# LSTM with a conditioned adapter on one core: adapter weights from contiguous columns of W2, bias added on VectorE and placed by transfers, two early blocks, end reordered

## What is computed

```python
def lstm(x, h0, Wx, Wh, b):            # x: 16 x 256 x 256
    xz = x @ Wx + b
    for t in range(256):
        ai, af, ao, ag = split(xz[:, t] + h @ Wh, 4)
        c = sigmoid(af) * c + sigmoid(ai) * tanh(ag)
        h = sigmoid(ao) * tanh(c)      # h is the output of step t
x = x + lstm(x, cond, Wx, Wh, b)

def adapter(x, cond, ...):
    c = layernorm(cond) * gamma + beta
    w = gelu(c @ W1 + bias1) @ W2 + bias2            # 16 x 8192
    a1, b1, a2, b2 = [t.reshape(16, 256, 8) for t in split(w, 4)]
    u   = einsum("btd,bdr->btr", x, a2)
    mid = gelu(x @ base_down + einsum("btr,blr->btl", u, b2))
    v   = einsum("blr,btl->btr", b1, mid)
    return mid @ base_up.T + einsum("bkr,btr->btk", a1, v)
x = x + adapter(x, cond, ...)
```

## Time and profile before

| | |
|---|---|
| median of three runs | 617.69 us (616.36 to 618.73) |
| profiled execution | 618.71 us, its span 616.9 us |
| granted TensorE clock, mean | 0.994 of full speed |
| PE, busy share of the span | 97% |
| DVE | 77% |
| ACT | 61% |
| POOL | 6% |
| mean DMA rate over the span | 63 GB/s |

### The profile page before, as it was taken

The page is one execution under the profiler, slowest core; times in us unless marked ns, Lnnn a source line. Parts: engine busy times, 40 slices in busy tenths (PEclk is TensorE's granted clock), DMA queues, the critical chain, the costliest instruction groups (busy, mean ns, idle before and its releaser), DMA issues.

```text
span 616.9 us, 33976 instructions
## 1 busy us (share of the span) xinstructions
PE 600.0 (97%) x14120; PEld 439.0 (71%) x14120; DVE 473.0 (77%) x2543; ACT 375.9 (61%) x2158; POOL 38.6 (6%) x77
## 2 busy tenths in 40 slices
PE   8699999999999999999999999999999999999997
PEld 5565555777777777777777777777777777777886
DVE  3576667888888888888888888888888888888772
ACT  2365555666666666666666666666666666666662
POOL 3000000000000000000000000000000000000000
PEclk9799999999999999999999999999999999999999
DMA  5884630233333113323221233322113323221201
GB/s 161 229 209 157 182 46 15 35 46 55 55 55 54 33 33 49 54 55 54 55 38 37 39 54 55 54 55 44 37 32 55 55 55 55 49 39 25 47 21 35
DMA packets 31499, 38.74 MB, mean 63 GB/s; under 512 B 3632, under 2 KB 29536, under 8 KB 30321
## 3 DMA queue, kind: packets, MB, share of 16 engines
q1 hardware_dynamic: 31282, 36.51, 29.8%
q0 software_dynamic: 64, 0.07, 0.0%
HBM read 15.59 MB, written 4.19 MB: 32 GB/s over the span
## 4 chain that ended last, share of the span: by engine, by line
PE 94%; DVE 2%; DMA 1%; issue 1%; ACT 0%; SPq 0%; ACTq 0%
PE z L696 36%; PE x_bank L494 18%; PE z_o L696 9%; PE aux L520 8%; PE out_bank L543 6%; PE out_bank L625 3%; PE aux L505 3%; PE aux L472 2%; PE out_bank L575 2%; PE aux L527 2%; PE out_bank L564 1%; PE x_bank L564 1%; DMA seed<-proj 1%; PE x_bank L520 1%; DVE z L833 0%
## 5 line engine op out<-in xcount | busy, mean ns | idle before, releaser
L696 PE MATMUL z<-wh,h_t 128*16 128x96 f32 x8160 | 236.5, 249 | 3.4 <-DVE h_t L853 2.0
L696 PEld LDWEIGHTS z<-wh,h_t 128*16 128x16 f32 x8160 | 154.0, 96 | 120.0 <-DVE h_t L853 86.5
L833 DVE STREAM_TRANSPOSE z<-z 128x96 f32<-128x96 f32 x512 | 151.4, 298 | 83.5 <-PE z L696 64.0
L413 ACT ACTIVATE gates<-z 128x48 f32<-128x48 f32 x512 | 107.2, 209 | 127.4 <-DVE z L833 127.3
L494 PE MATMUL x_bank<-wx,x_t 128*128 128x256 f32 x512 | 156.2, 393 | 0.5 <-ACT x_t L331 0.5
L337 ACT ACTIVATE z<-seed 128x96 f32<-128x96 f32 x512 | 127.7, 250 | 5.9 <-DMA seed<-proj 5.8
L696 PE MATMUL z_o<-wh,h_t 128*16 128x64 f32 x4080 | 104.1, 219 | 0.4 <-issue 0.4
L843 DVE SCALAR_TENSOR_TENSOR prod<-gates 128x32 f32<-128x32 f32 x512 | 97.6, 191 | 1.2 <-ACT gates L413 0.3
L341 ACT ACTIVATE z_o<-seed 128x64 f32<-128x64 f32 x256 | 58.3, 228 | 60.5 <-DVE h_t L853 60.5
L848 DVE SCALAR_TENSOR_TENSOR gates<-prod 128x16 f32<-128x16 f32 x512 | 84.3, 165 | 8.7
L494 PEld LDWEIGHTS x_bank<-wx,x_t 128*128 128x128 f32 x512 | 80.7, 195 | 6.4 <-issue 1.5
(11 more groups left out here) (114 smaller groups left out, 440.6 us busy)
## 6 DMA issues: line engine op xcount, KB each, us to landing
seed<-proj SPq DMA_DIRECT2D x128, 128.0 KB, 4.2
w<-in_L_cond_W SPq DMA_DIRECT2D x4, 2048.0 KB, 10.2
x_nat<-in_x SPq DMA_DIRECT2D x32, 128.0 KB, 4.3
out<-y_nat SPq DMA_DIRECT2D x32, 128.0 KB, 4.0
wx<-in_L_cond_Wx SPq DMA_DIRECT2D x2, 512.0 KB, 6.1
wh<-in_L_cond_Wh SPq DMA_DIRECT2D x2, 256.0 KB, 7.0
wh<-in_L_cond_Wh SPq DMA_DIRECT2D x1, 512.0 KB, 6.4
w<-in_L_cond_W SPq DMA_DIRECT2D x1, 256.0 KB, 4.5
```

The source lines that it names most:

```text
L413: act.activation(gates[s % 2][m][:, 0:3 * B].rearrange("p (g b) -> p g b", b=B), zt[m].rearrange("p (g c) -> p g c", c=C)[:, :, 0:B], ACT. ...
L696: ins = pe.matmul(dst, h_prev[:, kc, :], rhs, start=False, stop=(kc == 1), skip_group_check=True)
L833: dve.transpose(zt[m], z_bank[m][:, 0:GC]).then_inc(turned[m], 1)
```

## The change

Each quarter's weights are computed with sequence on the rows and 256 contiguous columns of W2 as moving operand: four steps a quarter (`NQ`), two halves of two contraction chunks, sixteen steps in all, from step 7 of block 0 on (`W_FIRST`). Bias2 is loaded by POOL at the start, spread over the rows of 16 sequences in four groups of partitions (`w_bias`). DVE adds it to each half of a quarter at even steps of blocks 1 and 2, writing with the rank outermost (`w_nat`). POOL then moves each quarter with four transfers onto the 128 partitions (`place_w`), in blocks 0 and 1 of its order behind `add_h`; PE waits for these transfers. Partitions are now (sequence, rank), and `own_row` follows. The order of the quarters changes and the transposes of two of them move to steps 0 and 4 of block 2. The halving of two operands moves into gelu's scale.

`EARLY` is 2, so follower jobs start in block 3, and no early job is left after block 31. The last follower job is written out anew, with both banks. SP's last load of W2 moves ahead of the seed of its block. Two waits move: ACT's for the seed from ahead of the first tanh of a block's last step to behind it, and DVE's for `add_h` from ahead of a block's first transpose to an earlier place in the block before (`h_free`).

Declarations, semaphores and the masks' new argument are left out of the diff.

```diff
@@ -38,11 +38,14 @@
 LN_EPS = 1e-5
-QUARTERS = (1, 2, 0, 3)
-W_STEPS = 5
-
-
-EARLY = 3
+QUARTERS = (2, 1, 3, 0)
+W_FIRST = 7
+W_COLS = D * RANK // NQ
+W_HALF = W_COLS // 2
+
+
+EARLY = 2
+W_PLACED = 16 * NQ
...
@@ -288,20 +291,20 @@
             load_seed(Blk(0, 1))
-            load_cols(down_raw, base_down, 0, 0, D, "down")
+            load_cols(down, base_down, 0, 0, D, "down")
                     load_w2(QUARTERS[1])
+                if k.k == 1:
+                    sp.wait_ge(w_psum, 2)
+                    load_w2(QUARTERS[3])
                 if front:
                     load_w2(QUARTERS[2])
-                if not k.at_least(2) and k.k == 1:
-                    sp.wait_ge(w_psum, 1)
-                    load_w2(QUARTERS[3])
                 done = follower(k.plus(-1))
...
@@ -346,7 +348,7 @@
                                mid_bank[a.lane][:, 0:2 * P].rearrange("p (l t) -> p l t", l=2),
-                               ACT.Gelu).then_inc(act_ready[a.lane], 1)
+                               ACT.Gelu, scale=0.5).then_inc(act_ready[a.lane], 1)
@@ -361,29 +363,15 @@
                     for i in range(2):
-                        act.activation(hid_win[:, i, B:2 * B], aux[:, i * B:(i + 1) * B], ACT.Gelu,
+                        act.activation(hid[:, i, :], aux[:, i * B:(i + 1) * B], ACT.Gelu,
                                        bias=b1_col[:, i:i + 1]).then_inc(hidden_ready, 1)
                     act.activation(up_t[:, s - 4, :], out_bank[:, 0:D], ACT.Copy).then_inc(up_ready, 1)
-                if 0 <= (k - 1) * TB + s < 4 * W_STEPS and ((k - 1) * TB + s) % W_STEPS == W_STEPS - 1:
-                    n = ((k - 1) * TB + s) // W_STEPS
-                    q = QUARTERS[n]
-                    act.wait_ge(w_psum, n + 1)
-                    src = out_bank[:, 0:D]
-                    if q == 0:
-                        ins = act.activation(a1_t[:, :], src, ACT.Copy)
-                    elif q == 1:
-                        ins = act.activation(w_tmp[:, 0, :], src, ACT.Copy)
-                    elif q == 2:
-                        ins = act.activation(w_tmp[:, 1, :], src, ACT.Copy, scale=0.5)
-                    else:
-                        ins = act.activation(b2_t[:, :], src, ACT.Copy)
-                    ins.then_inc(w_copied, 1)
-                if k == 2 and s in (2, 6):
+                if k == 2 and s in (0, 4):
                     n = s // 4
                     act.wait_ge(wt_psum, n + 1)
-                    act.activation((b1_w, a2_w)[n][:, :, :], aux[:, 0:2 * P].rearrange("p (l t) -> p l t", l=2),
+                    act.activation((a2_w, b1_w)[n][:, :, :], aux[:, 0:2 * P].rearrange("p (l t) -> p l t", l=2),
                                    ACT.Copy).then_inc(wt_ready, 1)
@@ -425,10 +413,10 @@
-                    if s == TB - 1 and more:
-                        act.wait_ge(seed_loaded[ahead.par], (ahead.turn + 1) * (16 * NQ))
                     gates_of(0)
                     if more:
+                        if s == TB - 1:
+                            act.wait_ge(seed_loaded[ahead.par], (ahead.turn + 1) * (16 * NQ))
                         seed_bank(ahead.par, s_next, 0)
@@ -457,9 +445,7 @@
             copy_y(follower(Blk(NBLK // 2 - 1, 1)))
-            gelu_mid(last_early)
             gelu_mid(last)
-            copy_y(last_early)
             copy_y(last)
@@ -511,8 +497,8 @@
                     if i == 0:
-                        pe.wait_ge(w_copied, 4)
-                        pe.wait_ge(down_ready, 1)
+                        pe.wait_ge(w_placed[3], W_PLACED)
+                        pe.wait_ge(w_loaded["down"], 16)
                         pe.wait_ge(u_ready[a.lane], a.seq.k + 1)
@@ -536,6 +522,7 @@
                         pe.wait_ge(up_ready, 2)
+                        pe.wait_ge(w_placed[0], W_PLACED)
                         pe.wait_ge(v_ready[a.lane], a.seq.k + 1)
@@ -601,34 +588,27 @@
                     ins.then_inc(up_psum, 1)
-                if 0 <= (k - 1) * TB + s < 4 * W_STEPS:
-
-
-                    n, i = divmod((k - 1) * TB + s, W_STEPS)
-                    q = QUARTERS[n]
+                if 0 <= k * TB + s - W_FIRST < 4 * NQ:
+
+
+                    n, i = divmod(k * TB + s - W_FIRST, NQ)
+                    q, (h, kc) = QUARTERS[n], divmod(i, 2)
                     if n == 0 and i == 0:
-                        pe.wait_ge(w_loaded["b2row"], 32)
-                        pe.wait_ge(window_made, 1)
                         pe.wait_ge(hidden_ready, 2)
                         pe.wait_ge(up_ready, 2)
-                    elif i == 0:
-                        pe.wait_ge(w_copied, n)
-                    if i == 1:
+                    elif kc == 0:
+                        pe.wait_ge(w_biased, 2 * n + h)
+                    if i == 0:
                         pe.wait_ge(w2_loaded[q], 16)
                     for j in range(NQ):
-                        if i == 0:
-                            lhs, rhs = one_win[:, :], b2_row[:, q, :].rearrange("p (d r) -> p r d", r=RANK)[:, 2 * j, :]
-                        else:
-                            odd, kc = divmod(i - 1, 2)
-                            lhs = hid_win[:, kc, (1 - odd) * B:(3 - odd) * B]
-                            rhs = w2[q][:, kc, :].rearrange("p (d r) -> p r d", r=RANK)[:, 2 * j + odd, :]
-                        ins = pe.matmul(out_bank[32 * j:32 * (j + 1), 0:D], lhs, rhs, start=(i == 0),
-                                        stop=(i == W_STEPS - 1))
-                    if i == W_STEPS - 1:
+                        first = W_COLS * j + W_HALF * h
+                        ins = pe.matmul(out_bank[32 * j:32 * j + B, 0:W_HALF], hid[:, kc, :],
+                                        w2[q][:, kc, first:first + W_HALF], start=(kc == 0), stop=(kc == 1))
+                    if kc == 1:
                         ins.then_inc(w_psum, 1)
-                if k == 2 and s in (2, 6):
+                if k == 2 and s in (0, 4):
                     n = s // 4
-                    pe.wait_ge(w_copied, n + 1)
+                    pe.wait_ge(w_placed[QUARTERS[n]], W_PLACED)
                     if n == 0:
@@ -701,13 +681,10 @@
                             transpose_y(done, (s - 3,))
-                    if s == 7 and not front and k.p == 1:
-                        pe.wait_ge(v_ready[1], last_early.seq.k)
-                        down_rank(last_early)
                     if s in x_steps and k.plus(3).exists():
                             pe.wait_ge(hidden_ready, 2)
-                        if k.at_least(EARLY - 1) and not k.at_least(EARLY):
+                        if k.k == 2:
                             pe.wait_ge(wt_ready, 2)
@@ -746,14 +723,36 @@
             schedule(one_block)
-            down_full(last_early, range(6))
-            down_rank(last)
-            up_rank(last_early)
-            down_full(last, range(6))
-            up_rows(last_early, ("l0", "x0", "x1"))
-            up_rank(last)
-            up_rows(last_early, ("l1", "v"), whole=True)
-            up_rows(last, ("l0", "x0", "x1", "l1", "v"), whole=True)
+            pe.wait_ge(v_ready[0], last.seq.k)
+            pe.wait_ge(v_ready[1], EARLY)
+            pe.wait_ge(xp_ready, last.blk.k * 2 + 2)
+            for m in both:
+                ins = pe.matmul(mid_bank[1][:, 0:P], a2_w[:, m, :], last.xp[:, m, :], start=(m == 0), stop=(m == 1))
+            ins.then_inc(u_psum[0], 1)
+            for part in range(3):
+                for l in range(2):
+                    cols = slice(l * P, (l + 1) * P)
+                    if part == 2 and l == 0:
+                        pe.wait_ge(u_ready[0], last.seq.k + 1)
+                    lhs, rhs = ((down[:, part, cols], last.xp[:, part, :]) if part < 2 else
+                                (b2_t[:, cols], u_own[0][:, :]))
+                    ins = pe.matmul(mid_bank[0][:, cols], lhs, rhs, start=(part == 0 and l == 0), stop=(part == 2),
+                                    skip_group_check=True)
+            ins.then_inc(mid_psum[0], 1)
+            pe.wait_ge(y_copied[0], last.seq.k)
+            for m in both:
+                pe.matmul(up_bank[0][:, m * P:(m + 1) * P], last.xp[:, m, :], ident[:, :], start=(m == 0), stop=False,
+                          skip_group_check=True)
+            pe.wait_ge(act_ready[0], last.seq.k + 1)
+            for l in range(2):
+                ins = pe.matmul(mid_bank[1][:, 0:P], b1_w[:, l, :], act_t[0][:, l, :], start=(l == 0), stop=(l == 1))
+            ins.then_inc(v_psum[0], 1)
+            for l in range(2):
+                pe.matmul(up_bank[0][:, 0:D], act_t[0][:, l, :], up_t[:, l, :], start=False, stop=False,
+                          skip_group_check=True)
+            pe.wait_ge(v_ready[0], last.seq.k + 1)
+            pe.matmul(up_bank[0][:, 0:D], v_own[0][:, :], a1_t[:, :], start=False, stop=True,
+                      skip_group_check=True).then_inc(y_psum[0], 1)
...
@@ -824,9 +822,7 @@
```

(71 more changed lines are left out.)

28 lines of the change are left out of this document (13 added, 15 removed).

## The result

The changed kernel takes 610.16 us (median; 608.51 to 610.4) against 617.67 of the kernel before on the same chip, a ratio of 0.9874 (95% interval 0.9855 to 0.9894). It is faster, as forecast, but by 7.5 us and not by 11.7. The profiled execution took 610.4 us, so its span stands for the median.

A forecast was written before the change was run, and what follows sets the result against it. The LSTM loop sets steps with short filling, PE the adapter-weight steps of blocks 1 to 3. Terms -7.1 (weights), -1.7 (moved waits) and -3.0 (end) make -11.8 us: 606 us, range 603 to 610.

The forecast's parts named there:

- Weight matmuls: TensorE's adapter-weight steps: contiguous W2 columns bring records near 385 ns and a 2.14 us step, under the loop's 2.225.
- rival 1: Column groups, not the stride, slow L625; weight steps stay at 2.55 us, 5.3 less gain, 611.2 us; chance 0.07.
- Blocks 1 to 3: Stretch with the adapter-weight work: 55.62 us in place of 62.88, a gain of 7.3.
- I keep 0.70 for it: Block 1's first step: z stops at 41.53, goes on at 42.26, releaser "issue"; 0.70 us kept in the sum.
- SP is through in time: zero: SP's order: W2's last part ahead of block 3's seed, which is ready some 11 us later; no cost.
- VectorE's add: Eight bias adds at even steps, 0.42 to 0.92 us each, hidden in VectorE's 0.48 us idle time: zero cost.
- Rival 2: The bias add's strided write is slow, 0.92 us: 609.4 us; chance 0.13.
- Placing by POOL: Sixteen POOL transfers, issues of 0.53 to 0.7 us; PE waits 0.5 to 1.2 us once in block 3, 0.8 taken.
- Rival 4: POOL's issues in series: at 2.6 us each the gain is gone, at 3.1 the time is 625.7; chance 0.04.
- The moved waits: Block boundaries: ScalarE's seed wait gives 0.06 us in 28 blocks, -1.7; VectorE's for add_h zero, at best 0.06 a block.
- Rival 3: The moved waits bring nothing, a wait costing its 0.06 us wherever it stands: 607.6 us; chance 0.13.
- The end: After the last LSTM step, without `last_early`: the last copy ends at 610.5 instead of 613.49, -3.0 us.

The follow-up runs named there:

- the stride kept: Changed kernel with the weight matmuls reading W2 in steps of 8 elements again, all else the same: 612.78 us, ratio 0.9912.
- three parts small: Changed kernel loading only 64 of 2048 columns of W2's second, third and fourth parts, all matmuls reading the first part's tile: 604.07 us, ratio 0.9778.
- 2 MB more: Kernel before, with W2's last part also loaded behind the third part into a tile nobody reads: 620.58 us, ratio 1.0034.
- pieces with two under way: Changed kernel, W2 in sixteen 0.5 MB transfers, at most two under way: 606.15 us; with place_w(3) behind add_h(2) as well: 606.95 us.
- the third part ahead of the seed: Changed kernel, W2 in 0.5 MB pieces, two under way, third part issued before block 2's seed, place_w(3) behind add_h(2): 610.34 us.
- the last part after the third: Changed kernel with SP loading W2's last part only once the third part has landed: 608.57 us, ratio 0.9857.

## Why the prediction was right in sign and short in size

- **Weight matmuls.** Right: 399 ns by records (385 forecast) and steps of 2.20 to 2.24 us (2.225). The kernel with the stride kept shows that the stride was the cause; rival 1 is out. The Trainium skill's sentence on lines (Advanced Engine Details and Errata, SBUF Cachelines) agrees with the trace here: 629 against 399 ns. One figure of the working is off: 0.9 ns a column make 230 ns of 256 columns, not 215, and so a record as long as L494's 393 ns; the step stays under the loop's 2.225 with either.
- **Blocks 1 to 3, the step that failed.** "I keep 0.70 for it" took the stall in block 1's first step for a constant. It was a wait for instructions, and the same trace has a second one, the 0.43 us above, that the prediction did not list. The stalls are now 0.66 (at the same place in PE's order, now in block 0), 1.32 and 1.93 us, with a spell at the lower clock behind them, and the loss is 4.9 us in blocks 1 to 3 and 0.7 in block 0. The text named such stalls among what would be wrong but gave them neither a price nor a chance. The second place is SP: the last part's load was costed by SP's order alone ("SP is through in time: zero"). SP was, but the DMA engines, which carry PE's instructions too, now had it at once with the third part. Without the loads, blocks 1 to 3 take 55.2 us (41.47 to 96.69), with 55.62 forecast, or 54.9 without the 0.70: the rest of the sum held to 0.3 us.
- **VectorE's add.** 0.62 us, between the bounds of 0.42 and 0.92, and hidden as forecast. The add starts 0.18 us after the second new h, and the next transpose, in the step after, follows its z by 0.71 us (49.80 to 50.51); with L765 in that place it is 0.69 (47.60 to 48.29). Rival 2 is out. The Trainium skill's lines point the right way for the write too, 0.62 against 0.42, but the trace's factor is 1.5 where 2.2 was the upper bound, no run changes the write alone, and it cost nothing here:

```profile
50.03 0.62 DVE L876 TENSOR_TENSOR w_nat<-out_bank,w_bias 128x256 f32<-128x256 f32 x1
50.51 0.63 DVE L829 STREAM_TRANSPOSE z<-z 128x96 f32<-128x96 f32 x2
```

- **Placing by POOL.** Right: issues of 0.54 us, and PE waited 0.99 us where 0.5 to 1.2 stood; 0.8 was taken. Rival 4, the other side, would have needed 2.6 us.
- **The moved waits.** ACT's was right, 0.06 us a block. "I count zero" for DVE's was wrong: it is worth as much. The step argued that PE waits for `add_h` and L505 in that step anyway. It does, but the z behind them also waits for the second half of h, and that came 0.06 us sooner. Rival 3 is out. Both together, with 28 blocks of 0.12, are 3.4 of the 4.1 us in that row. The other 0.7 lie in single blocks: four of the kernel before took 17.90 to 18.14 us, the longest with a stall of 0.18 us (issue) that ends at 290.38, and no run shows why the other three did.
- **The end.** Right: 3.5 us where 3.0 was forecast, of which 2.85 lie between `add_h` and the last copy (6.06 against 8.91).
- **The sum.** 5.6 us were lost to late instructions and the clock in blocks 0 to 3 and 0.6 before the first z; 2.9 more than forecast came from the moved waits and the end. That is the 3.3 us between 11.8 and 8.5 in the profiled executions. The time ended 0.16 us above the range. That it came so near is in part luck: DVE's wait, counted as zero for a wrong reason, gave 1.7 us of it.

What stays open: why a packet of instructions starts late in one kernel and not in another. The loads of W2 make the long stalls (three parts small, 2 MB more), though not every short one (0.42 us at 86.64 in the kernel with three small parts). Neither the amount queued nor the size of a transfer decides alone: pieces with two under way had no stall above 0.21 us in two kernels and three long ones with the third part ahead of the seed. Each of these traces is of one execution, and executions of one kernel lie up to 5 us apart (607.46 to 612.55 for the last part after the third). An order that is surely free of it was not found. The kernel with pieces has the lowest median of those that load all of W2, 606.15 us.

## What to carry to other kernels

When an edit makes an engine faster or moves a load closer to another, look for stalls with the releaser "issue" in the profile before: they are a price that grows, not a constant. A load that lands in time can still cost, since it shares the DMA engines with the instructions of the engine that it feeds. The runs show the place: PE stops only every 256 instructions, so the time from one such place to the next, and not the single matmul, is what to compare with a packet's arrival. And a wait that has long been met still took 0.06 us on ACT and on DVE where it stands on the loop, so it belongs where its engine is idle.

## What the runs showed of the hardware beyond what was expected

- PE's instructions come in packets of 16.4 KB, one for 256 instructions (28,661 records, 112 packets), some 5 us of this kernel's work. Beside W2's loads packets can come late, and then PE stood still for 0.2 to 2.7 us, each time 193 or 194 records above a multiple of 256.
- TensorE's clock can fall behind a stall. After PE had worked 2.07 of 4.00 us the granted clock was 0.72 in the next 4 us; in the kernel with more to load 3.17 of 4.00, then 0.61. It does not behind every stall: in the changed kernel PE worked 2.68 of 4.00 us from 50 to 54, and with the third part early 1.33 of 4.00 us from 70 to 74, and the clock stayed at 1.00 in the next 4 us.
- A transfer of POOL from 16 partitions to 128 took 6.7 us (median of four) to land beside W2's loads and 1.9 to 2.0 us for the three quarters placed later.
